# A fused audio-tower layer on one core: another order of work at the end, and one expert's weights loaded at another place

## The chip, the cores and the metric

The kernel runs on one core of one Trainium2 chip. The metric is the device time of one execution in microseconds (us), taken as the median of a few runs. A profile of one execution, taken by the hardware profiler, stands beside it.

## The reference, cut to what matters

The input is 64 clips, each cut to 7 patches of 16 x 64 values, so there are 448 tokens. Three stages follow.

```
h = layernorm(layernorm(patches) @ W + b)                    # 448 x 512
h = h + bitlinear(silu(gate) * value)                        # 512 -> 2 x 1408 -> 512, quantised
x = layernorm(h);  p = softmax(x @ router.T);  top 8 of 32 experts, shares normalised
h = h + sum over the chosen experts e of  share_e * (silu(x @ wg_e) * (x @ wu_e)) @ wd_e   # 512 -> 192 -> 512
```

The output is `h`, 448 x 512 in f32.

## The kernel before, in words

All matrices of the experts are in f32. The 448 tokens lie as 4 groups (g = 0 to 3) of 112 partitions. The work on the five engines is written out by hand as five instruction streams; every dependence is a semaphore wait, and each engine takes its stream strictly in order. SyncE (SP) and ScalarE (ACT) each issue direct DMAs on their own queue; GpSimd (POOL) issues the indexed gathers and scatters.

**Start and middle.** Patches, the first product and the quantised layer (up to about 97 us) end in `residual(g)` and `row(g)`: the normalised row of each token is stored to a DRAM table `token_rows`, 544 values per token, of which the last 32 are the token's shares. SP stores the four groups' rows (L511), waits for the shares (`gate_ready`), stores these (L513), then waits for `z_done` and for the first transposed tile (`xt_done` 1, L515) and loads experts 10 and 11 (`load_expert`, L487). Expert weights are 1,280 KB for an even expert and 1,024 KB for an odd one; there are 12 slots, and slot 10 lies over the matrix and the transposed values that the last product of the quantised layer reads (`z_done` tells that it has). POOL waits for all stores to `token_rows` (`rows_out` at 96) and issues the first gather (L646), with which the expert stage begins.

**Expert stage.** For each expert t = 0 to 31 a tile of up to 128 tokens is gathered, transposed, put through gate, up and down products, and added by a scatter with accumulate (L661) to one of two DRAM tables, `sum0` for even and `sum1` for odd t. A scatter waits until the scatter before it to the same table has landed (`added[n]`). Tokens of an expert beyond 128 are kept in lists of 32, four lists in a "quad", two quads a and b in a round. There is one round here (`n_pairs` is at least 1, and the loop of `pairs_of` runs once). The quads come after tile 31: PE does their products (L1186, L1218, L1220), ACT copies the result of each to SBUF (`y_list_out`, L892), and PE adds them into token order in PSUM by a product with a 0/1 matrix (`spread_lists`, L1243), a bank per group.

**The end before.** ACT's order in the round is: silu of both quads; wait until `added[0]` is complete, load all of `sum0` to SBUF (L917); wait until `added[1]` is complete, load all of `sum1` (L917); only then `y_list_out(a)` and `y_list_out(b)`. PE's `spread_lists` needs both copies in the order a, b within each group. DVE (VectorE) then does three adds for each group: `grown(g)` (L1751: h += PSUM bank g), `with_first(g)` (L1756: sum0 + h) and `finished(g)` (L1761: that + sum1 into `result`). SP stores groups 0 to 2 of the output and ACT group 3 (L446). PE's and ACT's work for a next round (`transpose_x`, `x_turned`) also stands at the end of the round.

Of the kernel before, what the change touches and what calls it, by code (L numbers as in the profile page):

```python
# [118 lines left out]
def program(nc, x, w_tok, vecs, gb1, w_in, w_down, g_down, w_router, ffn, out):  # L119
# [3 lines left out]
    with ctx:  # L123
# [3 lines left out]
        def sem(name):  # L127
            return ctx.enter_context(nc.semaphore(name))
# [141 lines left out]
        def bank(b, n=1):  # L270
            return ps[:, b:b + n, :].rearrange("p b c -> p (b c)")
# [60 lines left out]
        ld_rest = [sem(f"ld_rest{n}") for n in range(R)]  # L332
        ld_got = [sem(f"ld_got{n}") for n in range(8)]
        added = [sem(f"added{n}") for n in range(2)]
        ld_part = [sem(f"ld_part{n}") for n in range(2)]

        dve_chain = sem("dve_chain")
        pool_chain = sem("pool_chain")
# [66 lines left out]
        where_ready = sem("where_ready")  # L405
        spread_done = sem("spread_done")
        y_last = sem("y_last")
        with_h_ready = sem("with_h_ready")
        h_ready = sem("h_ready")

        place_done = sem("place_done")
# [11 lines left out]
        y_ready = sem("y_ready")  # L423
        fin_ready = sem("fin_ready")
        out_done = sem("out_done")
        act_out_done = sem("act_out_done")

        block = ctx.enter_context(nc.Block())
        ABS_COLS = (slice(0, 8), slice(8, 8 + DC))
# [9 lines left out]

        def bcast(v, n):  # L440
            return v.rearrange("(a n) -> a n", a=1).broadcast_to([G, n])

        def store(eng, g, n_pairs, done):

            eng.wait_ge(fin_ready, 4 * n_pairs + g)
            eng.dma_start(out_v[:, g, :], result[:, g, :]).then_inc(done, 16)  # L446


        @block.sync
        def _(sp):  # L450
            def load_x(g):
                sp.dma_start(xt[:, g, :], x_v[:, g, :]).then_inc(ld_x[g], 16)

            def load_down_piece(m):
                a, b = DOWN_PART[m], DOWN_PART[m + 1]
                sp.dma_start(w_down_raw[:, a:b, :], wdown_v[:, a:b, :]).then_inc(ld_wdown[m], 16)

            load_x(0)
            for n in range(2):
                sp.dma_start(raw_flat[:, n * 4 * D:(n + 1) * 4 * D],  # L460
                             w_tok.rearrange("(p c) n -> p (c n)", c=KC)[:, n * 4 * D:(n + 1) * 4 * D]
                             ).then_inc(ld_wtok[n], 16)
            for g in range(1, NG):
                load_x(g)

            def load_in_piece(n):
                a, b = WIN_PART[n], WIN_PART[n + 1]
                sp.dma_start(w_in_raw[:, a:b, :], win_v[:, a:b, :]).then_inc(ld_win[n], 16)

            for n in range(4):  # L470
                load_in_piece(n)
            for m in range(4):
                load_down_piece(m)
            sp.dma_start(gdn_bc[:, :], bcast(g_down, I1)).then_inc(ld_late, 16)
            sp.dma_start(rw_t[:, :, :], w_router.rearrange("p (c e) -> p c e", c=DC)).then_inc(ld_late, 16)
            sp.wait_ge(consts, 1)
            sp.dma_start(rows_dram[TOK:ROWS, :], zeros[:, :]).then_inc(rows_out, 16)
            for n in range(2):
                sp.dma_start(acc_dram[n][TOK:ROWS, :], zeros[:, 0:D]).then_inc(sums_ready, 16)
            for n in range(2):  # L480
                for g in range(NG):
                    sp.dma_start(acc_dram[n][g * G:(g + 1) * G, :], zeros[0:G, 0:D]).then_inc(sums_ready, 16)

            def load_expert(t):

                n, cols = t % R, WCOLS if t % 2 == 0 else WG + D
                sp.dma_start(slots[n][:, 0:cols], ffn[t, :, 0:cols]).then_inc(ld_gu[n], 16)  # L487

            def load_picked(e, n):

                sp.dma_start(slots[n][:, 0:WG + D], ffn[e, :, 0:WG + D]).then_inc(ld_gu[n], 16)
                sp.dma_start(down_rest_of(n), ffn[e, 0:IB, WG + D:WCOLS]).then_inc(ld_rest[n], 16)

            sp.wait_ge(t1_done, NG)
            load_expert(0)
            for t, signs in ((1, 3), (2, 5), (3, 8)):
                sp.wait_ge(wt_ready, signs)
                load_expert(t)
            sp.wait_ge(wd_ready, DC)
            for t in (4, 5, 6):  # L500
                load_expert(t)
            sp.wait_ge(swg_ready, gained(NG - 1))
            sp.wait_ge(swg_rest_ready, 1)
            sp.wait_ge(ssq2_ready, NG)
            load_expert(7)
            load_expert(8)
            sp.wait_ge(q2t_done, NG + 1)
            load_expert(9)
            for g in range(NG):
                sp.wait_ge(row_ready, g + 1)  # L510
                sp.dma_start(rows_v[:, g, 0:D], rows[:, g, 0:D]).then_inc(rows_out, 16)  # L511
            sp.wait_ge(gate_ready, NG)
            sp.dma_start(rows_v[:, :, D:ROW], rows[:, :, D:ROW]).then_inc(rows_out, 16)  # L513
            sp.wait_ge(z_done, NG)
            sp.wait_ge(xt_done, 1)  # L515
            load_expert(10)
            load_expert(11)
            for t in range(R, NE):
                sp.wait_ge(y_done, t - R + (1 if t % 2 else 2))
                load_expert(t)  # L520
            for k, n_pairs in pairs_of(sp, pairs_i, table_ready):
                for n in range(NLIST):
                    s = (NE + n) % R
                    e = sp.value_load(owner_row[0:1, bass.ds(NLIST * k + n, 1)], min_val=0, max_val=NE - 1)
                    sp.wait_ge(y_done, R * k + (NE - R + n + 1))
                    load_picked(bass.ds(e, 1), s)
            for g in range(NG - 1):
                store(sp, g, n_pairs, out_done)
            sp.wait_ge(out_done, 16 * (NG - 1))


        @block.gpsimd
        def _(pool):
# [144 lines left out]
            for k, n_pairs in pairs_of(pool, pairs_i, table_ready):  # L678
                for i in range(2):
                    gather(Quad(k + 1, i))  # L680
            for i in range(2):
                pool.wait_ge(ld_got[i], 16 * n_pairs + 16 * (NE // 8 + 1))

# [2 lines left out]
        def _(act):  # L686
# [222 lines left out]
            for k, n_pairs in pairs_of(act, pairs_i, table_ready):  # L909
                two = [Quad(k, 0), Quad(k, 1)]  # L910
                for m in two:
                    act.wait_ge(gu_done, m.lists(3))
                    silu(m)
                act.wait_ge(fin_ready, 4 * k + 3)
                for m in two:
                    act.wait_ge(added[m.i], 16 * (NE // 2))
                    act.dma_start(part[m.i][:, :, :], acc_v[m.i]).then_inc(ld_part[m.i], 16)  # L917
                for m in two:
                    y_list_out(m)
                for i in range(2):  # L920
                    x_turned(Quad(k + 1, i))
            store(act, NG - 1, n_pairs, act_out_done)
            act.wait_ge(act_out_done, 16)


        @block.tensor
        def _(pe):
# [307 lines left out]

            def spread_lists(two):

                for g in range(NG):
                    for m in two:
                        if g == 0:  # L1240
                            pe.wait_ge(y_ready, m.upto(-1))
                            pe.wait_ge(where_ready, 2 * m.k + (m.i + 1))
                        last = nc.tensor.matmul(bank(g)[0:G, :], where[:, m.i, g * G:(g + 1) * G], y_list[:, m.i, :],  # L1243
                                                start=m.i == 0, stop=m.i == 1)
                    last.then_inc(spread_done, 1)

            def list_starts():

# [76 lines left out]
        def _(dve):  # L1325
# [376 lines left out]
            for t in range(NE):  # L1702
# [13 lines left out]
                if t == 8:  # L1716
                    list_sought()
                    for i in range(2):
                        pick_lists(Quad(0, i))
                    nc.vector.tensor_copy(pairs_f[:, :], pairs_i[:, :]).then_inc(fin_ready, 3)  # L1720
                    dve.sem_inc(h_ready, 4)
                if t % 2 == 0:
                    turn_back(m)
# [6 lines left out]
            for k, n_pairs in pairs_of(dve, pairs_i, table_ready):  # L1730
# [19 lines left out]
                    dve.wait_ge(spread_done, 4 * k + (g + 1))  # L1750
                    nc.vector.tensor_tensor(h[:, g, :], h[:, g, :], bank(g)[0:G, :], ALU.add).then_inc(h_ready, 1)  # L1751

                def with_first(g):
                    dve.wait_ge(ld_part[0], 16 * k + 16)
                    dve.wait_ge(h_ready, 4 * k + (g + 5))
                    nc.vector.tensor_tensor(part[0][:, g, :], part[0][:, g, :], h[:, g, :], ALU.add).then_inc(with_h_ready, 1)  # L1756

                def finished(g):
                    dve.wait_ge(ld_part[1], 16 * k + 16)
                    dve.wait_ge(with_h_ready, 4 * k + (g + 1))  # L1760
                    nc.vector.tensor_tensor(result[:, g, :], part[0][:, g, :], part[1][:, g, :], ALU.add).then_inc(fin_ready, 1)  # L1761

                grown(0)
                with_first(0)
                grown(1)
                with_first(1)
                grown(2)
                with_first(2)
                finished(0)
                finished(1)  # L1770
                grown(3)
                with_first(3)
                finished(2)
                finished(3)


def laid_out(x, w_tok, b_tok, g1, b1, g2, b2, w_in, g_in, w_down, g_down, w_router, we_gate, we_up, we_down):
# [37 lines left out]
```

## Time and profile before

| | |
|---|---|
| median of 3 runs | 301.75 us |
| lowest, highest | 301.51, 305.46 us |
| the profiled execution, its own time | 302.17 us |
| its span, first to last instruction | 300.4 us |
| busy share of the span: TensorE, VectorE, ScalarE, GpSimd | 93%, 50%, 42%, 43% |
| mean granted TensorE clock over the span | 0.981 |

The span leaves out 1.77 us of the profiled execution's own time. A busy share is an average over stages that are limited by different things, so the stage at the end has to be read by its own rows. Times in the rows count from the start of the span.

### The profile page before, as it was taken

The numbers are of one execution on the slowest core, as the hardware profiler recorded it, in microseconds if no ns is written. First come the engines' busy times: TensorE is split into PE (matmuls) and PEld (weight loads), VectorE is DVE, ScalarE is ACT, GpSimd is POOL, SyncE is SP. The second block draws the span as 40 slices with busy tenths as digits, with TensorE's granted clock in tenths as the row PEclk, the third lists the DMA queues.
The fourth block names the chain that finished last, engine by engine and source line by source line (L and its number), as shares of the span: only waits on it lengthen the run. The fifth ranks groups of instructions, "written<-read, shape, count | busy, mean of one in ns | idle before, by whom it ended". The sixth has DMA issues, their size and how long they took to land.

```text
span 300.4 us, 3845 instructions
## 1 busy us (share of the span) xinstructions
PE 278.0 (93%) x1159; PEld 147.6 (49%) x1159; DVE 151.1 (50%) x446; ACT 125.2 (42%) x213; POOL 127.7 (43%) x130
## 2 busy tenths in 40 slices
PE   4899999869999988999999999999999999999792
PEld 1335444536557445546545655565555545553131
DVE  2657999997798705263343332333243223114345
ACT  2346999899984412213321332133213321331101
POOL 3162210976542133253546445654366436434400
PEclk9999999999999599999999999999999999999979
DMA  7999999501979087599999999999999999966773
GB/s 241 319 412 422 378 406 333 245 0 38 422 280 324 14 268 271 176 303 280 305 311 344 326 341 344 371 336 347 345 365 323 336 303 324 331 122 96 139 176 125
DMA packets 19478, 83.67 MB, mean 279 GB/s; under 512 B 3476, under 2 KB 3604, under 8 KB 13345
## 3 DMA queue, kind: packets, MB, share of 16 engines
q1 hardware_dynamic: 11440, 64.77, 57.5%
q0 software_dynamic: 7488, 16.58, 24.6%
q10 hardware_dynamic: 530, 2.08, 2.7%
q8 instruction: 10, 0.16, 0.2%
q14 instruction: 10, 0.08, 0.1%
HBM read 72.34 MB, written 12.92 MB: 284 GB/s over the span
## 4 chain that ended last, share of the span: by engine, by line
PE 35%; DMA 26%; DVE 18%; issue 5%; ACT 4%; POOL 1%; POOLq 0%; DVEq 0%; ACTq 0%
DMA sum<-w_t,add_idx 22%; PE ps L1174 16%; PE ps L1202 5%; PE ps L1195 3%; PE ps L1205 3%; DMA ring<-sum 3%; DVE big L1456 2%; DVE stats L1340 2%; PE ps L1061 2%; DVE raw L1462 2%; PE ps L1227 1%; DMA scrap<-token_rows,idx 1%; PE ps L1158 1%; DVE scrap L1421 1%; ACT last L814 1%
## 5 line engine op out<-in xcount | busy, mean ns | idle before, releaser
L661 POOL DMA_INDIRECT sum<-w_t,add_idx x32 | 51.3, 1602 | 55.6 <-ACT w_t L888 40.9
L877 ACT ACTIVATE w_t<-ps 128x512 f32<-128x512 f32 x36 | 21.3, 598 | 76.3 <-PE ps L1195 76.1
L648 POOL DMA_INDIRECT scrap<-token_rows,idx x28 | 29.5, 1053 | 28.6 <-DVE add_idx L1647 13.9
L1657 DVE COPY w_t<-ps 128x256 f32<-128x256 f32 x34 | 14.4, 424 | 53.6 <-PE ps L1230 52.4
L1652 DVE SCALAR_TENSOR_TENSOR w_t<-ps,scrap,w_t 128x192 f32<-128x192 f32 x32 | 13.2, 413 | 54.1 <-issue 44.9
L882 ACT ACTIVATE w_t<-ps 128x192 f32<-128x192 f32 x34 | 11.3, 331 | 54.2 <-PE ps L1174 48.8
L1174 PE MATMUL ps<-ring,w_t 128*128 128x384 f32 x96 | 33.1, 487 | 0.7 <-ACT w_t L877 0.7
L566 POOL TENSOR_TENSOR root_out<-root_in,minus_half 112x1 f32<-112x1 f32 x20 | 13.1, 654 | 46.6 <-DVE root_in L1357 46.6
L965 PE MATMUL ps<-raw,last 128*112 128x512 f32 x64 | 31.3, 643 | 0.0
L1174 PE MATMUL ps<-big,w_t 128*128 128x384 f32 x88 | 30.2, 486 | 0.0
L1195 PE MATMUL ps<-ident,scrap 128*128 128x128 f32 x144 | 23.0, 284 | 2.1 <-DVE h L1751 1.8
L1195 PEld LDWEIGHTS ps<-ident,scrap 128*128 128x128 f32 x144 | 21.1, 206 | 7.3 <-issue 6.0
L1174 PEld LDWEIGHTS ps<-ring,w_t 128*128 128x128 f32 x96 | 17.4, 192 | 10.4 <-ACT w_t L877 0.9
L1638 DVE SCALAR_TENSOR_TENSOR hit<-ps,iota_p,token 128x448 f16<-128x448 f32 x32 | 21.6, 676 | 1.4 <-PE ps L1263 1.0
L1023 PE MATMUL ps<-w_t,scrap 128*112 128x512 bf16 (+1 forms) x96 | 20.5, 363 | 1.7 <-DVE raw L1462 1.2
L888 ACT ACTIVATE w_t<-ps 128x512 f32<-128x512 f32 x31 | 17.4, 597 | 9.1 <-PE ps L1205 5.5
L965 PEld LDWEIGHTS ps<-raw,last 128*112 128x112 f32 x64 | 11.8, 192 | 18.4 <-issue 18.4
L1174 PEld LDWEIGHTS ps<-big,w_t 128*128 128x128 f32 x88 | 16.0, 191 | 8.7
L577 POOL TENSOR_TENSOR big<-raw,scrap 112x704 f32<-112x704 f32 (+1 forms) x7 | 12.7, 1825 | 8.7 <-DVE raw L1462 8.7
L1023 PEld LDWEIGHTS ps<-w_t,scrap 128*112 128x112 bf16 x96 | 11.9, 130 | 8.5 <-DVE raw L1462 1.4
L646 POOL DMA_INDIRECT scrap<-token_rows,idx x8 | 7.8, 979 | 17.5 <-DVE idx L1641 10.5
L723 ACT ACTIVATE scrap<-big 128x1536 bf16<-128x1536 f32 (+1 forms) x8 | 11.0, 1378 | 6.7 <-DMA big<-in_mlp_w_in 6.2
(216 smaller groups left out, 472.7 us busy)
## 6 DMA issues: line engine op xcount, KB each, us to landing
big<-in_ffn SPq DMA_DIRECT2D x12, 1024.0 KB, 9.3
ring<-in_ffn SPq DMA_DIRECT2D x9, 1280.0 KB, 7.5
ring<-in_ffn SPq DMA_DIRECT2D x4, 1024.0 KB, 9.9
raw<-in_ffn SPq DMA_DIRECT2D x4, 1024.0 KB, 9.0
last<-in_ffn SPq DMA_DIRECT2D x4, 1024.0 KB, 10.1
big<-in_ffn SPq DMA_DIRECT2D x3, 1280.0 KB, 8.0
big<-in_mlp_w_in SPq DMA_DIRECT2D x2, 1536.0 KB, 18.1
big<-in_mlp_w_in SPq DMA_DIRECT2D x2, 1280.0 KB, 20.7
```

Source lines behind the costliest of these rows:

```text
L648: nc.gpsimd.indirect_dma_start(got[:, got_at(s), :], None, rows_dram[:, :], rows_, bounds_check=TOK - 1, oob_is_err=False).then_inc(ld_got ...
L661: nc.gpsimd.indirect_dma_start(acc_dram[m.two][:, :], bass.IndirectOffsetOnAxis(ap=add_idx[:, m.eight:m.eight + 1], axis=0), y[:, m.four, ...
L877: nc.scalar.activation(x_t[:, m.two, :, :], bank(2 + m.two).rearrange("p (c t) -> p c t", c=4), ACT.Copy).then_inc(xt_ready, 1)
L888: nc.scalar.activation(y[:, m.four, :], bank(4 + m.two), ACT.Copy).then_inc(y_ready, 1)
L965: last = nc.tensor.matmul(acc, patch_t[g % 2][:, c, :], wtok_raw[:, c, :], start=False, stop=c == KC - 1)
L1023: last = nc.tensor.matmul(bank(3 * half_, 3)[0:G, a:a + w], q1_t[:, c, g * G:(g + 1) * G], w_t4[:, c, half_ * I1 + a:half_ * I1 + a + w], ...
L1174: last = nc.tensor.matmul(dst, x_t[:, m.two, c, :], wg[:, :, c, :], start=c == 0, stop=c == 3)
L1195: last = nc.tensor.transpose(bank(2 + m.two)[:, c * P:(c + 1) * P], got[:, got_at(m.eight), c:D:4], ident[:, :])
L1202: nc.tensor.matmul(bank(4 + m.two), h_t[:, m.two, 0, :], down_of(m.slot), start=True, stop=False)
L1638: nc.vector.scalar_tensor_tensor(hit[:, :], bank(b)[:, 0:TOK], mine, token[:, :], ALU.is_equal, ALU.mult, accum_out=idx_f[:, s:s + 1]).the ...
L1652: nc.vector.scalar_tensor_tensor(hid[:, m.two, 0:IE], bank(m.two)[:, IE:2 * IE], gate, sg[:, :], ALU.mult, ALU.mult).then_inc(hid_ready, 1)
L1657: nc.vector.tensor_copy(h_t[:, m.two, :, :], bank(6)[:, 0:2 * P].rearrange("p (c t) -> p c t", c=2)).then_inc(ht_ready, 1)
```

## The change

Five things are different.

1. ACT no longer waits for the sums and no longer loads them: after silu it goes to `y_list_out(a)` and `y_list_out(b)`.
2. SP loads the sums, in four pieces of 224 KB for each table (one per group), after `added[n]` is complete. Each piece has its own semaphore, `ld_part[n][g]`.
3. POOL adds the two sums for each group (part0 + part1), once both pieces of that group have landed and after its last two gathers. DVE does `grown(g)` for all four groups, and after the round, for each group, one add of POOL's sum and h into `result`. All four stores of the output are SP's.
4. PE's spreading takes the products in the order (group, quad) = (0,a) (1,a) (0,b) (2,a) (1,b) (3,a) (2,b) (3,b), in place of a, b for each group in turn.
5. SP waits for `z_done` and loads expert 10 after the four row stores, ahead of the wait for the shares, their store and the wait for `xt_done`. Expert 11 stays behind `xt_done`.

A small DVE copy that made up the count of `fin_ready` at tile 8 is gone.

```diff
@@ SP
             for g in range(NG):
                 sp.wait_ge(row_ready, g + 1)
                 sp.dma_start(rows_v[:, g, 0:D], rows[:, g, 0:D]).then_inc(rows_out, 16)
+            sp.wait_ge(z_done, NG)
+            load_expert(10)
             sp.wait_ge(gate_ready, NG)
             sp.dma_start(rows_v[:, :, D:ROW], rows[:, :, D:ROW]).then_inc(rows_out, 16)
-            sp.wait_ge(z_done, NG)
             sp.wait_ge(xt_done, 1)
-            load_expert(10)
             load_expert(11)
...
-            for g in range(NG - 1):
-                store(sp, g, n_pairs, out_done)
-            sp.wait_ge(out_done, 16 * (NG - 1))
+            for n in range(2):
+                sp.wait_ge(added[n], 16 * (NE // 2))
+                for g in range(NG):
+                    sp.dma_start(part[n][:, g, :], acc_v[n][:, g, :]).then_inc(ld_part[n][g], 16)
+            for g in range(NG):
+                sp.wait_ge(fin_ready, g + 1)
+                sp.dma_start(out_v[:, g, :], result[:, g, :]).then_inc(out_done, 16)
+            sp.wait_ge(out_done, 16 * NG)
@@ POOL
+            for g in range(NG):
+                for n in range(2):
+                    pool.wait_ge(ld_part[n][g], 16)
+                nc.gpsimd.tensor_tensor(part[0][:, g, :], part[0][:, g, :], part[1][:, g, :], ALU.add).then_inc(both_ready, 1)
@@ ACT
-                act.wait_ge(fin_ready, 4 * k + 3)
-                for m in two:
-                    act.wait_ge(added[m.i], 16 * (NE // 2))
-                    act.dma_start(part[m.i][:, :, :], acc_v[m.i]).then_inc(ld_part[m.i], 16)
                 for m in two:
                     y_list_out(m)
...
-            store(act, NG - 1, n_pairs, act_out_done)
-            act.wait_ge(act_out_done, 16)
@@ PE
-                for g in range(NG):
-                    for m in two:
-                        if g == 0:
...
+                for g, i in ((0, 0), (1, 0), (0, 1), (2, 0), (1, 1), (3, 0), (2, 1), (3, 1)):
+                    m = two[i]
+                    if g == 0:
...
+                    if m.i == 1:
+                        last.then_inc(spread_done, 1)
@@ DVE
-                grown(0)
-                with_first(0)
-                grown(1)
-                with_first(1)
-                grown(2)
-                with_first(2)
-                finished(0)
-                finished(1)
-                grown(3)
-                with_first(3)
-                finished(2)
-                finished(3)
+                for g in range(NG):
+                    grown(g)
+            for g in range(NG):
+                dve.wait_ge(both_ready, g + 1)
+                dve.wait_ge(h_ready, 4 * n_pairs + (g + 1))
+                nc.vector.tensor_tensor(result[:, g, :], part[0][:, g, :], h[:, g, :], ALU.add).then_inc(fin_ready, 1)
```

## Rows read from the trace of the kernel before

**Rows 1.** The page's head.

```profile
span 300.4 us, 3845 instructions
```

**Rows 2.** Chain that ended last, 260 to 301 us: start, length, what.

```profile
276.94 4.81 DMA sum<-w_t,add_idx
...
281.83 8.06 DMA ring<-sum
...
293.86 0.69 DVE raw L1761
```

**Rows 3.** Timeline, 281.5 to 301 us: start, length, engine, line, operation, [idle before, releaser].

```profile
281.83 2.17 ACTq L917 DMA_DIRECT2D ring<-sum  x2
...
282.52 0.34 PE L1165 MATMUL ps<-w_t,pick 32*128 32x448 f16 x1
...
284.05 1.08 ACT L892 ACTIVATE scrap<-ps 128x512 f32<-128x512 f32 x2 [5.94 <-DMA sum<-w_t,add_idx]
...
284.77 8.81 PE L1243 MATMUL ps<-scrap,ranked 128*112 128x512 f32 x16 [1.91 <-ACT scrap L892]
284.94 1.04 POOL L648 DMA_INDIRECT scrap<-token_rows,idx  x1 [2.21 <-DVE idx L1641]
...
287.66 0.69 DVE L1751 TENSOR_TENSOR h<-h,ps 112x512 f32<-112x512 f32 x1 [3.68 <-PE ps L1243]
...
295.78 1.28 DVE L1761 TENSOR_TENSOR raw<-ring 112x512 f32<-112x512 f32 x2
...
297.10 0.33 ACTq L446 DMA_DIRECT2D out<-raw  x1
```

**Rows 4.** L917, the loads of the sums: issues, then time to landing.

```profile
L917 ACTq DMA_DIRECT2D ring<-sum x2: 320/336/351, 281.8 to 283.7; - x2
...
DMA to landing us min/median/max: 8.1/8.6/9.1
```

**Rows 5.** L446, the four stores of 224 KB to the output: time to landing.

```profile
DMA to landing us min/median/max: 2.3/2.8/3.0
```

**Rows 6.** Windows: stretch, length, PE, PEld, DVE, ACT, POOL busy, PEclk, DMA share, GB/s.

```profile
284.00:286.00 2.00, 1.23 (x3) 0.73 (x4) 0.00 (x0) 1.08 (x2) 1.04 (x1) 0.93 0.93 275
286.00:288.00 2.00, 2.00 (x3) 0.64 (x3) 0.34 (x1) 0.00 (x0) 0.00 (x0) 0.50 0.90 213
288.00:290.00 2.00, 2.00 (x5) 0.68 (x4) 0.35 (x2) 0.00 (x0) 0.00 (x0) 0.72 1.02 266
```

**Rows 7.** GpSimd's adds or products of two SBUF tensors: L577, durations in ns.

```profile
L577 POOL TENSOR_TENSOR big<-raw,scrap x7: 1671/1683/2315, 61.6 to 81.8; 112x704 f32<-112x704 f32 x6, 112x640 f32<-112x640 f32 x1
```

**Rows 8.** Timeline at 61 to 66 us and at 82 us: GpSimd and VectorE beside each other.

```profile
61.56 3.69 POOL L577 TENSOR_TENSOR big<-raw,scrap 112x704 f32<-112x704 f32 x2 [0.23 <-DVE raw L1462]
...
63.60 1.93 DVE L1437 TENSOR_SCALAR scrap<-scrap,fscale 112x512 f32<-112x512 f32 x1
...
81.81 0.96 DVE L1476 TENSOR_TENSOR big<-raw,scrap 112x768 f32<-112x768 f32 x1
...
81.85 2.31 POOL L577 TENSOR_TENSOR big<-raw,scrap 112x640 f32<-112x640 f32 x1 [3.65 <-DVE raw L1462]
```

**Rows 9.** Timeline, 89 to 109 us: SP's queue and the first gather.

```profile
89.93 6.46 SPq L511 DMA_DIRECT2D token_rows<-scrap  x4
...
100.32 0.72 SPq L513 DMA_DIRECT2D token_rows<-scrap  x1
...
103.51 1.21 POOL L646 DMA_INDIRECT scrap<-token_rows,idx  x1 [7.76 <-DVE idx L1641]
...
108.03 0.83 SPq L487 DMA_DIRECT2D last<-in_ffn  x2
```

**Rows 10.** L513, the store of the shares: time to landing.

```profile
DMA to landing us min/median/max: 2.2/2.2/2.2
```

**Rows 11.** Windows around SP's stores, columns as in rows 6.

```profile
88.00:90.00 2.00, 1.91 (x20) 1.25 (x19) 1.73 (x6) 1.91 (x4) 0.55 (x1) 1.00 1.00 411
98.00:100.00 2.00, 1.96 (x10) 0.97 (x10) 1.57 (x10) 0.88 (x5) 0.00 (x0) 0.50 0.02 8
```

More of the change, by code:

```diff
@@ L334, in program @@
         added = [sem(f"added{n}") for n in range(2)]
-        ld_part = [sem(f"ld_part{n}") for n in range(2)]
+        ld_part = [[sem(f"ld_part{n}_{g}") for g in range(NG)] for n in range(2)]
         dve_chain = sem("dve_chain")
@@ L407, in program @@
         y_last = sem("y_last")
-        with_h_ready = sem("with_h_ready")
+        both_ready = sem("both_ready")
         h_ready = sem("h_ready")
@@ L425, in program @@
         out_done = sem("out_done")
-        act_out_done = sem("act_out_done")
         block = ctx.enter_context(nc.Block())
@@ L441, in bcast @@
             return v.rearrange("(a n) -> a n", a=1).broadcast_to([G, n])
-        def store(eng, g, n_pairs, done):
-            eng.wait_ge(fin_ready, 4 * n_pairs + g)
-            eng.dma_start(out_v[:, g, :], result[:, g, :]).then_inc(done, 16)
         @block.sync
@@ L1236, in spread_lists @@
             def spread_lists(two):
-                for g in range(NG):
-                    for m in two:
-                        if g == 0:
[L1241 to L1245, printed above, removed]
+                for g, i in ((0, 0), (1, 0), (0, 1), (2, 0), (1, 1), (3, 0), (2, 1), (3, 1)):
+                    m = two[i]
+                    if g == 0:
+                        pe.wait_ge(y_ready, m.upto(-1))
+                        pe.wait_ge(where_ready, 2 * m.k + (m.i + 1))
+                    last = nc.tensor.matmul(bank(g)[0:G, :], where[:, m.i, g * G:(g + 1) * G], y_list[:, m.i, :],
+                                            start=m.i == 0, stop=m.i == 1)
+                    if m.i == 1:
+                        last.then_inc(spread_done, 1)
             def list_starts():
@@ L1719, in _ @@
                         pick_lists(Quad(0, i))
-                    nc.vector.tensor_copy(pairs_f[:, :], pairs_i[:, :]).then_inc(fin_ready, 3)
                     dve.sem_inc(h_ready, 4)
@@ L1751, in grown @@
                     nc.vector.tensor_tensor(h[:, g, :], h[:, g, :], bank(g)[0:G, :], ALU.add).then_inc(h_ready, 1)
[L1753 to L1761, printed above, removed]
-                grown(0)
-                with_first(0)
-                grown(1)
-                with_first(1)
-                grown(2)
-                with_first(2)
-                finished(0)
-                finished(1)
-                grown(3)
-                with_first(3)
-                finished(2)
-                finished(3)
+                for g in range(NG):
[4 more added lines that the diff above has]
+                nc.vector.tensor_tensor(result[:, g, :], part[0][:, g, :], h[:, g, :], ALU.add).then_inc(fin_ready, 1)
 def laid_out(x, w_tok, b_tok, g1, b1, g2, b2, w_in, g_in, w_down, g_down, w_router, we_gate, we_up, we_down):
```

## The prediction, written before the result was known

> **What bounds the kernel now.** I read the page's head first, then the chain that ended last for the final 40 us, then the timeline of the same stretch, and last the windows and the DMA rows. The span is 300.4 us [rows 1]. The chain at the end shows that no compute engine sets it: a scatter issued at 276.94 lands at 281.75, the load of the first sum is issued at 281.83 and lands 8.06 us later at 289.89, and then DVE adds one after the other [rows 2]. The second load is issued at 283.7 and lands 9.1 us later, at 292.8 [rows 4]. DVE's last add ends at 297.06, ACT's store is issued at 297.10 [rows 3], lands about 2.9 us later [rows 5], and 0.4 us are left to the end. So from 281.8 on the path is: sums from DRAM, what is left to add, a store. The spreading runs beside it. PE finishes the quads' products at 282.86 but starts spreading at 284.77, since ACT sat 5.94 us and copied the first quad only at 284.05 [rows 3]. That is the wait which the change takes away, and it lies beside the loads, not ahead of them.
>
> **Part 1, ACT's wait goes (copies and spreading).** The spreading starts at about 282.9, when PE is through, 1.9 us earlier [rows 3]. With the new order quad b is wanted first after two products, 2 x 8.81/8 = 2.2 us later at most, and ACT's copy, half of the 1.08 us that two take, is long done. The eight products took 8.81 us, of which the clock was at the low level for 3.4 us: the windows show 0.93, 0.50 and 0.72 over 6 us [rows 6], a loss of 1.7 us. Ahead of the fall PE had stood idle 1.9 us, which now goes, so I take the full level: 7.1 us, done at 290.0 (low level again: 291.7). `grown(3)` follows with 0.1 + 0.69 us [rows 3], at 290.8 (292.5). Gain on the path: nothing, as long as the sums come later. It is a floor, though: the final adds stand behind `grown(3)` in DVE's order, four at 0.69 us make 293.6 (295.3), and 0.1 for SP's reaction, 2.9 for the store and 0.4 to the end give 297.0 (298.7). No saving of more than 3.4 us can come of the end.
>
> **Part 2, the loads in pieces on SP.** The releasers are the same scatters at the same times, so piece 0 of sum0 still goes out at 281.8 and piece 0 of sum1 at 283.7. SP's direct DMAs cost about 0.35 us each to issue (ACT's 0.32 to 0.35 [rows 4]), four take 1.4 us and fit between the two. What decides is when piece (1,0), the fifth of eight, lands. Early bound: 283.7 + 2.6, as a store of this size takes alone [rows 5], 286.3. Late bound: the bytes keep the pace of before, half in at 289.89 and all at 292.8, so the fifth eighth at 289.89 + 2.9/4 = 290.6 [rows 2, 4]. Between: from 284 to 290 the queues moved 275, 213 and 266 GB/s, mean 251 [rows 6]; five pieces of 224 KB (1.147 MB) take 4.6 us, from 284.0, so 288.6. I take 288.6, for it is these bytes in this stretch without the wait for later bytes of the same load.
>
> The Trainium skill, "DMA: Bandwidth & Descriptors", section "Measured (HBM→SBUF, 128 partitions, SWDGE, issued from GpSimd)", speaks against pieces: it asks for 1 MiB or more in a DMA and shows 64 KB at 138 GB/s where 1 MB has 341. What I weigh of it here is that the loads of 896 KB were no faster than 251 GB/s either, while 224 KB stores landed in 2.3 to 3.0 us. By the page the pieces would land nearer the late bound, about 2 us more than my sum.
>
> **Part 3, GpSimd adds the sums.** POOL is free at 286.0, after its last gather [rows 3]. Products of two SBUF tensors of 704 columns took 1.683 us in the median [rows 7], 2.39 ns a column, so 1.22 us for 512, and 4.9 us for four. They run beside DVE's final adds, which read two SBUF tensors as well. Once in the trace the two met like this: POOL's 640 columns beside a DVE add of 0.96 us took 2.31 us in place of 1.53, 0.78 more [rows 8]. For a DVE add of 0.69 us that is 0.56, and three of them overlap: 1.7 us (bounds 0 and 3 x 0.69 = 2.1). DVE can lose as well: a 512-column operation took 1.93 us beside two POOL products [rows 8].
>
> Sum from the landing of piece (1,0): 0.1 reaction + 4.9 + 1.7 + 0.1 + 0.69 (DVE's last) + 0.1 (SP) + 2.9 + 0.4 = 10.9 us. 288.6 + 10.9 = 299.5 against 300.4: 0.9 us less. Late bound 290.6 + 10.9 = 301.5, early bound the floor of part 1.
>
> The Trainium skill, "SBUF — State Buffer", section "SBUF: two separate sides", calls this an exclusive lock: whichever of the two starts first holds the pair for its whole instruction. The 0.78 us beside a 0.96 us DVE add, and DVE's 1.93 us, are on its side. By it DVE's four final adds could all come behind POOL's four, 4.9 + 4 x 0.69 = 7.7 where I have 7.4 with the last add, 0.3 us more.
>
> **Part 4, expert 10 sooner.** SP has issued the fourth row store at 96.4 [rows 9], `z_done` is past by then (the fourth row is made from the residual that waited for it), so the load goes out there, behind the stores on the same queue. These are through by 98: the window 98 to 100 shows 8 GB/s [rows 11]. 1.31 MB at the 411 GB/s of 88 to 90 take 3.2 us, until 101.2. The store of the shares, issued at 100.32, landed 2.2 us later [rows 9, 10]; it now starts up to 0.9 us late if it had begun at once, and hardly late if its 0.72 us of issue and its start filled that time. POOL's first gather came 1.0 us after that landing [rows 9, 10], so a delay goes straight to it and to everything after. I take 0.1 us. Bounds: 0, and 2.0 if the load moves only at the 251 GB/s of part 2, 5.2 us, to 103.2, where the store would else have begun by 101.2. What it gives back: 1,280 KB fewer at 108, where PE waits for no DMA; nothing. SP's issue, 0.4 us, fits before the shares are ready at 100.3. The DVE copy that is gone has one element, and DVE is no bound there: nothing.
>
> **Sum.** -0.9 + 0.1 = -0.8 us on the profiled execution's 302.17, which is 0.42 above the median of 301.75. Predicted median: 300.9 us.
>
> **Rivals.**
> - *Forecast*, the pieces in the middle, GpSimd's adds the path: 299.5 to 302, chance 0.50.
> - *Fast pieces.* The pieces land near 286.5 to 287 and POOL and DVE don't collide: 287 + 9.2 = 296.2, so the floor decides, 297.0, or 298.7 at the low clock. Then the gain is 3.4 or 1.7 us: 298.3 or 300.0. For it: 224 KB stores alone land in 2.6 us. Against: the loads of before were slow from a queue that was busy 0.90 to 1.02 of the time [rows 6]. Chance 0.25.
> - *Slower: GpSimd becomes the end.* Piece (1,0) at 290.6 and POOL's adds at its dearest row, 2.31/640 a column, 1.85 us each: 7.4 in place of 6.6, so 301.5 + 0.8 = 302.3, 1.9 us above: 303.6. It decides as soon as piece (1,0) lands later than 289.5 with the collision as summed, since the rest takes 10.9. Chance 0.17.
> - *Shares behind the load.* The gather waits 2.0 us and takes back more than the end gives: 301.75 - 0.9 + 2.0 = 302.8; chance 0.08. By the same skill page, section "Queues, rings and completion order", SP's DMAs share rings and are taken in order, which the wait for the load's bytes here rests on.
>
> That the change does not do what it says is hardly open: ACT's wait stands ahead of both copies in its stream, and it is gone.
>
> **Range and chances.** The range 298.3 to 303.2 reaches from the floor at full clock to just under the slower rival's far end, and leaves out about 2 in 10. A measurement of this kernel can tell some 2% (6 us) from no change. Faster by over 2% would need an end before 294.4, below the floor: 0.03. Slower by over 2% needs both slow rivals and more: 0.03. Within 2%: 0.94.
>
> **What would show it.** Right: ACT's copies done by 283.3 with no DMA wait; spreading from 282.9 to 290; SP issuing eight loads between 281.8 and 285.2, with piece (1,0) landing near 288.6; POOL adds of 1.2 to 1.8 us; SP's last store near 296.1; the first gather near 103.6. Wrong: a spreading that ends after 291 or keeps the low clock (part 1), POOL adds above 2 us or waiting on pieces past 290 (parts 2, 3), DVE's final adds bunched behind POOL's last (the lock), the first gather past 104 (part 4), or tiles that take another time than before, which I hold unchanged.

## The result and the profile after

The changed kernel is **0.8% slower**: the ratio of comparable runs is 1.0084, 95% interval [1.0047, 1.012], which on 301.75 us is 2.5 us (1.4 to 3.6). The median of 20 runs was 305.5 us against 301.8 for the kernel before, one beside the other; single runs of either scatter over 7 us. (The ratio leaves disturbed executions out, the medians do not, which is why they lie further apart; the profiles of the first and third experiments below are of such disturbed executions, so their distances are read only beside those of others.) The forecast was 300.9 us, range 298.3 to 303.2, so both the sign and the range were missed.

The profiled execution of the changed kernel took 302.52 us, span 300.5, so beside [rows 1] it hardly shows the loss: this execution happened to be 1.2 us ahead already at 88 us, before anything that was changed. Spans of single executions are therefore no measure here. What follows compares *distances between two events of one execution*: from the issue of the load (or first piece) of sum1 to the end of the span, and from the index of the first tile to the first gather.

The chain of waits that ended last, from 276 us (start, length, what), answers to [rows 2]:

```profile
278.50 4.60 DMA sum<-w_t,add_idx
283.11 0.02 issue
283.12 5.54 DMA ring<-sum
...
288.80 1.28 POOL ring L682
...
290.27 1.10 DVE raw L1754
...
291.77 1.28 DVE raw L1754
...
293.44 1.27 DVE raw L1754
294.72 0.09 issue
294.80 0.99 DVEq L123
```

The first piece of sum1 landed at 283.12 + 5.54 = 288.66 (forecast 288.6), GpSimd began its adds 0.14 us later, and VectorE followed. The timeline of the same stretch (start, length, engine, line, operation), answering to [rows 3]:

```profile
280.42 0.60 ACT L894 ACTIVATE scrap<-ps 128x512 f32<-128x512 f32 x1 [2.60 <-PE ps L1216]
280.92 4.11 SPq L523 DMA_DIRECT2D ring<-sum  x8
...
282.41 0.60 ACT L894 ACTIVATE scrap<-ps 128x512 f32<-128x512 f32 x1 [1.39 <-PE ps L1216]
282.51 0.27 PEld L1239 LDWEIGHTS ps<-scrap,ranked 128*112 128x112 f32 x2 [0.21 <-issue]
...
288.80 5.83 POOL L682 TENSOR_TENSOR ring<-ring 112x512 f32<-112x512 f32 x4 [3.10 <-DMA ring<-sum]
...
289.67 0.69 DVE L1747 TENSOR_TENSOR h<-h,ps 112x512 f32<-112x512 f32 x1 [0.17 <-PE ps L1239]
290.27 5.52 DVE L1754 TENSOR_TENSOR raw<-ring,h 112x512 f32<-112x512 f32 x4
...
291.87 4.26 SPq L526 DMA_DIRECT2D out<-raw  x4
```

ScalarE's two copies wait for TensorE alone, and the spreading starts at 282.51, as soon as TensorE is through with its products: the first copy has been there since 281.02. Single lines: the loads in pieces, the stores, GpSimd's adds and VectorE's last adds (durations in ns, min/median/max, first to last start; then the time to landing), which answer to [rows 4, 5, 7]:

```profile
L523 SPq DMA_DIRECT2D ring<-sum x8: 303/427/620, 280.9 to 284.4; - x8
...
DMA to landing us min/median/max: 3.8/5.5/6.2
...
L526 SPq DMA_DIRECT2D out<-raw x4: 317/320/323, 291.9 to 295.8; - x4
...
DMA to landing us min/median/max: 2.3/2.3/2.6
...
L682 POOL TENSOR_TENSOR ring<-ring x4: 1267/1492/1715, 288.8 to 292.9; 112x512 f32<-112x512 f32 x4
...
L1754 DVE TENSOR_TENSOR raw<-ring,h x4: 678/1658/1749, 290.3 to 295.1; 112x512 f32<-112x512 f32 x4
```

The last store was issued at 295.82 and landed 2.6 us later, at 298.4. Yet the span ends at 300.5. What stands there is seen only when the instructions of the closing line L123 are asked for on GpSimd:

```profile
L123 POOLq COMPARE_BRANCH  x1: 41/41/41, 290.8 to 290.8; - x1
L123 POOLq DRAIN  x1: 9286/9286/9286, 291.0 to 291.0; - x1
```

and, the same two lines of the kernel before:

```profile
L123 POOLq COMPARE_BRANCH  x1: 41/41/41, 293.1 to 293.1; - x1
L123 POOLq DRAIN  x1: 5626/5626/5626, 293.2 to 293.2; - x1
```

Each of the five engines has such a DRAIN at the end of its stream, and in all 13 profiles of this text the span ends 0.21 to 0.25 us after the last of the five is over, whichever engine's that is. Before, GpSimd's DRAIN took 5.63 us and ended at 298.88, 1.5 us ahead of the end of the span. Now it starts while GpSimd's adds still run and ends at 300.29, which is 5.66 us after the end of the last add (294.63) and 0.2 us before the end of the span. SyncE's waits (us in all, times, longest) say the same from the other side, under its own closing line: after its last store has landed it waits 1.9 us for the others, where it waited 0.7 before. Where no closing of GpSimd stands in the way (the third, sixth, seventh, eighth, ninth and tenth experiments), 0.4 us lie between the last landing and the end of the span.

```profile
SPq L123 <- DMA out<-raw: 2.2, 1, 2.2
SPq L123 <- PEq L123: 1.9, 1, 1.9
```

Two more places, by windows (length; PE, PEld, VectorE, ScalarE, GpSimd busy; clock; DMA share; GB/s), which answer to [rows 6, 11]: first the load of expert 10 in its new place, then the end.

```profile
96.00:98.00 2.00, 1.84 (x10) 1.78 (x11) 1.20 (x9) 1.09 (x7) 0.00 (x0) 0.50 1.01 306
98.00:100.00 2.00, 1.63 (x10) 0.57 (x8) 1.51 (x10) 0.98 (x4) 0.00 (x0) 0.50 0.95 399
100.00:102.00 2.00, 1.78 (x5) 0.57 (x6) 1.16 (x4) 1.64 (x3) 0.00 (x0) 0.50 0.27 63
...
284.00:286.00 2.00, 2.00 (x6) 0.78 (x5) 0.62 (x1) 0.00 (x0) 1.04 (x1) 1.00 0.90 268
286.00:288.00 2.00, 2.00 (x6) 0.89 (x5) 0.76 (x2) 0.00 (x0) 0.00 (x0) 1.00 0.92 282
...
290.00:292.00 2.00, 1.23 (x8) 1.04 (x8) 2.00 (x3) 0.64 (x2) 2.00 (x3) 1.00 0.00 1
```

The queues, which before moved 8 GB/s from 98 to 100, now move 399, and the store of the shares, issued at 99.67 into this, lands later than the 2.2 us of [rows 10]. Expert 10's load, issued at 95.24, lands at 102.19, the shares at 102.56 and the first gather starts at 103.51. The load, and then the store:

```profile
L480 SPq DMA_DIRECT2D last<-in_ffn x1: 429/429/429, 95.2 to 95.2; - x1
...
DMA to landing us min/median/max: 7.0/7.0/7.0
```

```profile
L508 SPq DMA_DIRECT2D token_rows<-scrap x1: 715/715/715, 99.7 to 99.7; - x1
...
DMA to landing us min/median/max: 2.9/2.9/2.9
```

### The profile page after: what moved, and what is told of

Same layout as the page of the kernel before. It is cut to its first block, busy times and chain, and to the rows that moved or that the text cites. A ratio compares the mean times of both kernels' runs of the same rounds, so it can differ in the third digit from the quotient of the medians.

```text
span 300.5 us, 3841 instructions
## 1 busy us (share of the span) xinstructions
PE 276.6 (92%) x1159; PEld 147.5 (49%) x1159; DVE 151.4 (50%) x441; ACT 125.1 (42%) x213; POOL 133.7 (44%) x134
## 4 chain that ended last, share of the span: by engine, by line
DMA 36%; PE 24%; DVE 18%; issue 6%; ACT 4%; POOL 2%; DVEq 0%; POOLq 0%; ACTq 0%
DMA sum<-w_t,add_idx 34%; PE ps L1170 10%; PE ps L1198 3%; DVE big L1453 2%; DVE stats L1337 2%; PE ps L1191 2%; DMA ring<-sum 2%; PE ps L1201 2%; PE ps L1057 2%; PE ps L936 2%; DVE raw L1459 2%; DVE raw L1754 1%; ACT w_t L890 1%; DVE scrap L1418 1%; ACT last L816 1%
## 5 line engine op out<-in xcount | busy, mean ns | idle before, releaser
L884 ACT ACTIVATE w_t<-ps 128x192 f32<-128x192 f32 x34 | 11.3, 331 | 54.9 <-PE ps L1170 49.7
L961 PE MATMUL ps<-raw,last 128*112 128x512 f32 x64 | 30.2, 624 | 0.0
L644 POOL DMA_INDIRECT scrap<-token_rows,idx x8 | 7.8, 981 | 18.6 <-DVE idx L1638 11.3
```

What stands on the lines that cost most here:

```text
L961: last = nc.tensor.matmul(acc, patch_t[g % 2][:, c, :], wtok_raw[:, c, :], start=False, stop=c == KC - 1)
```

## The experiments

Two theories stood against each other for the loss. **The closing of GpSimd:** its late adds push its DRAIN past the last store. **The shares:** the store waits behind expert 10's bytes, and the whole expert stage starts later. Times are ratios to the kernel before on the same chip, with 95% intervals; "end" is the distance from the issue of sum1's first load to the start of the span's last instruction, 0.05 us before the end of the span (before: 16.67 us; changed: 17.36, and 17.19 in a second profile), "start" is from the end of the operation that makes the first tile's index on VectorE to the first gather (before: 1.11 us; changed: 1.76 and 2.06).

**Expert 10 back in its old place, the rest as changed.**

```diff
-            sp.wait_ge(z_done, NG)
-            load_expert(10)
             sp.wait_ge(gate_ready, NG)
             sp.dma_start(rows_v[:, :, D:ROW], rows[:, :, D:ROW]).then_inc(rows_out, 16)
+            sp.wait_ge(z_done, NG)
             sp.wait_ge(xt_done, 1)
+            load_expert(10)
```

> The changed kernel with one part undone: expert 10 is loaded where it was before, behind the first transposed tile; the new end is kept. Theory A (the load ahead of the shares' store held that store, 2.9 us to landing in place of 2.2, and with it the first gather by 0.7 us): faster than the changed kernel by about 0.7 us, the shares' store again 2.2 us to landing. Rival (the load's place is worth nothing, all of the loss is at the end): no difference to the changed kernel, first gather 1.8 us after the first index as there.

Measured: 0.9962 [0.991, 1.0013]; end 18.14, start 1.11, the store of the shares lands in 2.2 us again. The start is mended, and the end is not: GpSimd's last add and the DRAIN still close it (DRAIN until 304.86, span 305.1). The gain on the changed kernel's 1.0084 is 1.2 points, some 3.7 us on another chip, where 0.7 us was expected.

**The kernel before with only expert 10 moved.**

```diff
+            sp.wait_ge(z_done, NG)
+            load_expert(10)
             sp.wait_ge(gate_ready, NG)
             sp.dma_start(rows_v[:, :, D:ROW], rows[:, :, D:ROW]).then_inc(rows_out, 16)
-            sp.wait_ge(z_done, NG)
             sp.wait_ge(xt_done, 1)
-            load_expert(10)
```

> The kernel before with one part of the change alone: expert 10 loaded ahead of the wait for the shares. Theory A: about 0.7 us slower than before (302.5 where before is 301.8), with the shares' store landing 2.9 us after its issue. Rival: within 0.2 us of before.

Measured: 1.0013 [0.996, 1.0065]; start 1.40, the shares land in 2.5 us; end 16.99. In this profile the move costs 0.3 us by this distance, less than the 0.7 expected, and by time alone it cannot be told from nothing.

This run showed something about part 1 as well. It has ScalarE's wait and the same idle time ahead of the spreading (1.87 us; 1.91 in [rows 3]), but its clock did not fall, and the old order of the products took 7.12 us:

```profile
284.00:286.00 2.00, 1.32 (x3) 0.63 (x4) 0.00 (x0) 1.04 (x2) 1.04 (x1) 1.00 0.92 266
286.00:288.00 2.00, 2.00 (x6) 0.89 (x5) 0.69 (x1) 0.00 (x0) 0.00 (x0) 1.00 0.94 238
288.00:290.00 2.00, 2.00 (x6) 0.79 (x5) 0.00 (x0) 0.00 (x0) 0.00 (x0) 1.00 0.90 213
```

**As changed, but VectorE adds the two sums.**

```diff
@@ POOL
-            for g in range(NG):
-                for n in range(2):
-                    pool.wait_ge(ld_part[n][g], 16)
-                nc.gpsimd.tensor_tensor(part[0][:, g, :], part[0][:, g, :], part[1][:, g, :], ALU.add).then_inc(both_ready, 1)
@@ DVE
             for g in range(NG):
+                for n in range(2):
+                    dve.wait_ge(ld_part[n][g], 16)
+                nc.vector.tensor_tensor(part[0][:, g, :], part[0][:, g, :], part[1][:, g, :], ALU.add).then_inc(both_ready, 1)
                 dve.wait_ge(both_ready, g + 1)
```

> The changed kernel with the four adds of the two sums moved from GpSimd to VectorE, after the four adds of the spread products; all else as in the changed kernel. Theory B (the end waits for GpSimd's closing drain, which ends 5.66 us after GpSimd's last work, at 300.3, while the last store has landed by 298.1): with GpSimd free of the adds its drain starts when the last gathers have landed (about 290 to 291) and ends by 297; VectorE has eight adds of 0.69 us from 290.4, ends at 295.9, and the end is at about 298.7 where the changed kernel has 300.5, 1.8 us less. Rival C (only the collision of the two engines' adds costs, the drain is a record without effect): VectorE ends at 295.9 as it does now (295.8), so the end stays at 300.5, no difference.

Measured: 1.0005 [0.9956, 1.0054]; end 15.18, start 2.65. VectorE's last add ends 12.37 us after the issue of sum1's load, where it was 12.67 with GpSimd's help in the changed kernel: four adds more on VectorE cost no time there. They take 0.684 us each; beside GpSimd VectorE's adds took 1.66 and GpSimd's 1.49 in the median. And GpSimd's DRAIN is out of the way: issued at 299.11, over at 304.74, 1.5 us ahead of the end of the span.

```profile
L123 POOLq DRAIN  x1: 5626/5626/5626, 299.1 to 299.1; - x1
```

The start is the dearest seen. In this execution the bytes of expert 10 moved for longer after the store was issued, 236 GB/s from 100 to 102 where the profile of the changed kernel had 63; the load landed at 103.92, and the store, 3.8 us after its issue, at 104.26:

```profile
L508 SPq DMA_DIRECT2D token_rows<-scrap x1: 718/718/718, 100.5 to 100.5; - x1
...
DMA to landing us min/median/max: 3.8/3.8/3.8
```

**The kernel before with one late column on GpSimd.** One add of 112 x 1, which waits until VectorE has finished all four groups; its result is used by nothing.

```diff
@@ POOL
+            pool.wait_ge(fin_ready, 7)
+            nc.gpsimd.tensor_tensor(root_out[:, 0:1], root_in[:, 0:1], minus_half[:, :], ALU.add)
```

> The kernel before with one thing added: a one-column add on GpSimd (0.1 us, nobody reads it) that waits until three of the four final results are there, at about 296.5. Theory B: GpSimd's closing drain then ends about 5.6 us later, at 302.2 or more, and the kernel is some 2 us slower than before. Rival C: the tiny add is beside ScalarE's last store and the end stays where it is, no difference to before.

Measured: 1.0045 [0.9983, 1.0107]; end 19.83, 3.2 us more than before, for an add of 0.19 us. The timeline's last row and the closing line of GpSimd:

```profile
298.52 0.19 POOL L682 TENSOR_TENSOR root_out<-root_in,minus_half 112x1 f32<-112x1 f32 x1 [11.46 <-DVE raw L1763]
```

```profile
L123 POOLq DRAIN  x1: 5626/5626/5626, 298.8 to 298.8; - x1
```

The DRAIN ends at 304.44 and the span at 304.7. The duration is the same to the nanosecond as before and with VectorE's adds, though the last work ahead of it is one column here and a gather there. 5.73 us lie from the end of the add (298.71) to the end of the DRAIN, as 5.66 did behind the four large adds. So the size of the last work, 512 columns or one, made no difference of over 0.1 us. In the trace this settles the mechanism; in time the interval still holds 1.

**The changed kernel again, beside the next three.**

> The changed kernel once more, as it is, beside the others of this call. Theory B (GpSimd's closing drain sets the end): from the issue of the first load of sum1 to the end of the span 17 to 18 us again (17.4 in its first profile, 16.7 in the kernel before), and the drain's end within 0.3 us of the span's. Theory A: the first gather 1.4 us or more after the first index (1.1 in the kernel before).

Measured: 1.0052 [0.9998, 1.0107]; end 17.19, start 2.06, shares landing in 3.2 us. It agrees with the result.

**Both undone: expert 10 in its old place and VectorE adding the sums** (the edits of the first and the third experiment together).

> The changed kernel with both suspected costs gone: the sums are added by VectorE and not by GpSimd, and expert 10 is loaded at its old place. Theories A and B together: 1.5 us from load to end are won at the end (15.2 us as in the run with VectorE's adds alone, against 16.7) and the first gather comes 1.1 us after the first index, so about 1.5 us faster than before. Rival (the loss is somewhere in the expert stage, by another timing of its transfers): no faster than before.

Measured: 0.9897 [0.9829, 0.9965]; end 15.42, start 1.11. So what is left of the change (ScalarE's wait gone, loads and stores on SyncE, the new order of the products, none of them tried alone) is a gain, of 1.0% where about 1.5 us, 0.5%, was expected. The four variants form a square: changed 1.0052, without GpSimd's adds 1.0005, with expert 10 back 0.9962, with both 0.9897. Each edit gives 0.5 to 0.7% and 0.9 to 1.1%, whichever is made first (two of the four from another chip, so this is a reading of points whose intervals overlap).

**The loads whole.** The kernel before, with SyncE issuing both loads of 896 KB and all stores, ScalarE free of them, the new order of the products, and VectorE adding in the order four times `grown`, four times `with_first`, four times `finished`.

```diff
@@ SP
+                sp.wait_ge(fin_ready, 4 * k + 3)
+                for n in range(2):
+                    sp.wait_ge(added[n], 16 * (NE // 2))
+                    sp.dma_start(part[n][:, :, :], acc_v[n]).then_inc(ld_part[n], 16)
@@ ACT
-                act.wait_ge(fin_ready, 4 * k + 3)
-                for m in two:
-                    act.wait_ge(added[m.i], 16 * (NE // 2))
-                    act.dma_start(part[m.i][:, :, :], acc_v[m.i]).then_inc(ld_part[m.i], 16)
```

> The kernel before with ScalarE's wait gone and the new spreading order, but the sums loaded by SyncE in the two loads of 896 KB of before; VectorE does all adds, the four of the products first; expert 10 at its old place. It tells what the pieces are worth. If pieces land no earlier than their share of the whole (my late bound): the same as the run with VectorE's adds in pieces, 15.2 us from load to end. If whole loads land at 8.1 and 9.1 us as before and pieces sooner (5.5 to 6.6 us to the fifth piece in the traces so far): VectorE starts its eight adds at 6.2 us after that load's issue, ends at 11.8, and the end is at 14.7 us, so the pieces are worth nothing here.

Measured: 0.9895 [0.9826, 0.9964]; end 15.12. The two loads land in 7.7 and 8.6 us. That is as good as pieces with the sums added by VectorE (15.18 and 15.42), but the order of the adds differs too, so the pieces are not isolated. In this order they could give nothing: the adds of sum1 come last, from 292.80 on, and find the whole load landed at 292.2.

**Pieces, and VectorE's adds laid between.** As the last one, but with the four pieces of each load and the order grown 0, first 0, grown 1, first 1, grown 2, first 2, grown 3, finished 0, first 3, finished 1, 2, 3. The wait for the last gathers' landing goes from GpSimd to SyncE.

```diff
@@ SP
+                for n in range(2):
+                    sp.wait_ge(added[n], 16 * (NE // 2))
+                    for g in range(NG):
+                        sp.dma_start(part[n][:, g, :], acc_v[n][:, g, :]).then_inc(ld_part[n][g], 16)
+            for i in range(2):
+                sp.wait_ge(ld_got[i], 16 * (NE // 8 + 2))
@@ DVE
                 with_first(2)
-                finished(0)
-                finished(1)
                 grown(3)
+                finished(0)
                 with_first(3)
+                finished(1)
                 finished(2)
```

> The version the runs point to: pieces on SyncE, sum0 added to h by VectorE between the adds of the spread products, sum1 last, nothing on GpSimd after its last gather (the wait for that gather is SyncE's), expert 10 at its old place. Theory B: VectorE's last add ends 11.3 us after the first load of sum1 is issued, the end is at 14.2 us, 2.5 us less than before; GpSimd's drain starts when its last gather is issued and is over by 292. Rival C (the end follows the transfers alone, whoever adds): no better than the run with VectorE's adds behind the spreading.

Measured: 0.9847 [0.9768, 0.9925], from four executions; end 13.67, start 1.11. VectorE's timeline shows why it is shorter: the adds of sum0 fill its waits for TensorE, and only five are left behind the last `grown`.

```profile
288.59 0.69 DVE L1756 TENSOR_TENSOR ring<-ring,h 112x512 f32<-112x512 f32 x1
289.58 0.69 DVE L1751 TENSOR_TENSOR h<-h,ps 112x512 f32<-112x512 f32 x1 [0.30 <-PE ps L1242]
290.31 0.69 DVE L1756 TENSOR_TENSOR ring<-ring,h 112x512 f32<-112x512 f32 x1
290.92 0.68 DVE L1751 TENSOR_TENSOR h<-h,ps 112x512 f32<-112x512 f32 x1
291.51 0.69 DVE L1761 TENSOR_TENSOR raw<-ring 112x512 f32<-112x512 f32 x1
292.12 0.69 DVE L1756 TENSOR_TENSOR ring<-ring,h 112x512 f32<-112x512 f32 x1
292.72 1.89 DVE L1761 TENSOR_TENSOR raw<-ring 112x512 f32<-112x512 f32 x3
```

GpSimd's DRAIN ends at 293.97, 4.1 us before the end, and 2 us later than the 292 that was expected; it was not over until 2.83 us after the last gather had landed (291.14):

```profile
L123 POOLq DRAIN  x1: 8611/8611/8611, 285.4 to 285.4; - x1
```

**The same kernel on another chip, and with each suspect put back alone.**

> The best version so far (pieces on SyncE, all adds interleaved on VectorE, nothing late on GpSimd, expert 10 at its old place), as it is, with more runs. All theories: 0.98 to 0.99 of the time of the kernel before, about 13.7 us from the first load of sum1 to the end of the span.

Measured: 0.9878 [0.9816, 0.9939]; end 13.73, start 1.11. The version is 1.2 to 1.5% faster than the kernel before, on two chips, and so beats both kernels.

To it, expert 10's load was moved ahead of the shares (the edit of the second experiment):

> The best version with the one part of the change that is at the start of the expert stage: expert 10 loaded ahead of the shares' store. Theory A: the first gather comes 1.4 to 2.7 us after the first index (1.11 in the best version) and the kernel is 0.3 to 1.5 us slower than the best version. Rival (no cost): 1.11 us again, same time.

Measured: 0.9972 [0.9915, 1.0029]; start 1.92, shares landing in 3.1 us; end 13.88. The end is as good as without it, and most of the gain is gone, 0.94 points.

And to it, the one late column on GpSimd (the edit of the fourth):

> The best version with a one-column add on GpSimd (nobody reads it) that waits until three of the four final results are there. Theory B: GpSimd's closing drain ends 5.7 us behind that add, at about 300 where the best version ends at 298, and the stretch from the first load of sum1 to the end grows from 13.7 to about 16 us: 2 us slower. Rival C: no difference.

Measured: 1.0028 [0.9985, 1.0072]; start 1.11; end 16.59, 2.9 us more than the 13.73 beside it. The DRAIN, issued at 297.37, ends at 303.24, and the span at 303.5. Here the time shows it too: 1.5 points, with intervals that lie apart.

## Why the prediction was wrong, step by step

**What bounds the end: right as far as the last store.** From the landing of the first piece of sum1 to the issue of the last store I summed 7.6 us (0.1 + 4.9 + 1.7 + 0.1 + 0.69 + 0.1); it took 295.82 - 288.66 = 7.16.

**Part 1: right, with a reason too strong.** Spreading 282.51 to 289.63 at full clock, 7.12 us (forecast 282.9, 7.1, 290.0). But the idle time ahead of it does not by itself bring the fall of the clock: with 1.9 us of it the clock fell in the kernel before and in the fourth experiment and stayed up in the second. In the ten profiles without it the clock never fell there. That there is no gain on the path from this alone was right for the changed kernel. The floor was right as well: 297.0 was 13.3 us from the issue of sum1's load, and the eighth, ninth and tenth experiments, with VectorE's adds laid between, reached 13.67, 13.73 and 13.88.

**Part 2: right at the end, by some luck.** Piece (1,0) landed at 288.66, forecast 288.6. But its load went out at 283.12, 0.6 us sooner than I had it, and took 5.54 us where 4.9 was forecast (4.6 to 6.3 in the eight other profiles with pieces); the two errors cancel. The queues moved 268 and 282 GB/s from 284 to 288, where [rows 6] have 275 and 213. The rule of the Trainium skill, "DMA: Bandwidth & Descriptors", section "Measured (HBM→SBUF, 128 partitions, SWDGE, issued from GpSimd)", from which I had estimated that the pieces would cost about 2 us, is not borne out for these direct loads: the eight pieces had all landed 9.6 to 10.5 us after the first was issued (nine profiles), the two whole loads 10.7 to 11.3 us (four profiles).

**Part 3: the adds right, the end of the program left out. This is the step that failed.** GpSimd's first add took 1.27 us (forecast 1.22 alone), the four 5.83 (forecast 6.6 with collision); VectorE, not GpSimd, then paid for most of the collision. After 290, where both have work, both are busy the whole of 290 to 292, and VectorE's add goes from 0.68 to between 1.57 and 1.75 us. The Trainium skill, "SBUF — State Buffer", section "SBUF: two separate sides", describes an exclusive lock between the two; the trace agrees in kind. GpSimd's first two adds keep their 1.27 us, and VectorE's first, begun beside the second, takes 1.57 in place of 0.68; from then on the two engines take turns, GpSimd's adds 1.71 us and VectorE's 1.75, one pair every 1.67 us, a little less than the 1.27 + 0.68 = 1.95 us of the two alone. What failed is the phrase "2.9 for the store and 0.4 to the end". The store landed at 298.4, and by that phrase the end would have been at 298.8; it came at 300.5, because GpSimd's closing ran until 300.29. So up to the store the forecast gain was there: 15.7 us from the issue of sum1's load against 16.7 before. The closing took back 1.7 us. The row that tells of it stands in the trace of the kernel before: a DRAIN of 5626 ns that ended 1.5 us ahead of the end of the span. I had read [rows 3] and the chain [rows 2], and neither shows an instruction that is not counted as busy. From it the sum would have been: GpSimd's last add ends at 288.6 + 0.1 + 6.6 = 295.3, plus 5.6 and 0.2, gives 301.1 in place of 299.5, and thus a time 0.7 us above the profiled one. So the rival "GpSimd becomes the end" came true in sign, by another mechanism than its own: not dear adds but what follows the last of them.

**Part 4: mis-sized.** The shares' store was late by 0.7, 1.6, 1.0, 0.3 and 0.8 us in the five profiles with the early load (the changed kernel, the third, fifth, second and tenth experiments), on average 0.9, and the gather with it: in all 13 profiles it starts 0.94 or 0.95 us after the shares have landed. I had taken 0.1 with bounds of 0 and 2.0. I asked when the load's bytes would be through, and had 101.2 from the windows; what counted was when the load *landed*. That was 6.6 to 7.7 us after its issue, at 102.16 to 103.92, and the shares landed 0.33 to 0.37 us behind it in every one of the five. The rate in the window from 100 to 102 does not order the delays (63 GB/s with 2.9 us to landing, 212 with 2.5, 236 with 3.8, 405 with 3.1), the landing of the load does. The Trainium skill, "DMA: Bandwidth & Descriptors", section "Queues, rings and completion order", has descriptors of one ring taken in order; the constant 0.33 to 0.37 us agrees.

**The account.** End: 17.28 on average (17.36 and 17.19) against 16.67 and, in the second experiment, 16.99: +0.3 to +0.6 us, where -0.9 was forecast. Start: +0.65 and +0.95 us, where +0.1 was. Together 0.9 to 1.6 us of a measured 2.5 (1.4 to 3.6). Put into the forecast, GpSimd's closing alone makes 301.75 + 0.7 = 302.4, still inside the range; with 0.9 for the shares it is 303.3, just past its end at 303.2, and the measured ratio stands for 304.3. So the range was missed by both steps together and by something more. "Start" counts from an index that is itself late in some of these profiles. From the start of GpSimd's last one-column operation ahead of it (94.78 before, 93.58 changed) the first gather comes after 8.6 to 9.2 us in the eight profiles without the early load, on average 8.8, and after 9.6 to 10.7 in the five with it: 9.9 and 10.2 in those of the changed kernel. Counted so, the start costs 1.1 and 1.4 us and the whole 1.4 to 2.0. About 0.3 us of it lie ahead of the issue of the shares' store, and no run shows that the load causes them. The end is shown in trace and, on the best version, in time. Of the start, the lateness of the shares behind the load is shown; but putting the early load back costs some 1% in three comparisons of ratios (0.9, 1.1 and 0.9 points, about 2.9 us, each interval wide), two to three times what the gather was late, and 0.1% in the comparison within the kernel before. From the first gather to sum1's load the profiles with the early load took 179.6 to 185.9 us and those without 180.2 to 183.7, so the traces show no further loss and cannot exclude one of 1 to 2 us. This stays open.

## What to carry to other kernels

Ask each engine's closing instructions, not only its busy ones, how long they take: here GpSimd's last add, of 512 columns or of one, fixes the earliest end of the program 5.9 to 6.0 us later, so nothing late belongs on it, and a free engine is not free there. Before giving work to a second engine to relieve VectorE, look whether VectorE's own waits hold it: twelve adds laid between those waits were done 10.2 to 10.6 us after the issue of sum1's load, eight beside GpSimd after 12.5 to 13.5. And do not put a large load ahead of a small store that a whole stage waits for, even if the queue is empty for those microseconds: the store landed only behind the load.

## What the runs showed of the hardware that I had not expected

- **GpSimd's closing DRAIN lasts 5.63 us** when the engine was idle (5626 ns in the kernel before and in five of the experiments), and ends 5.66 us after the last add when it was issued while adds still ran (three profiles). Behind a last gather, with no wait for its landing, it ended 2.83 us after the gather had landed (three profiles).
- **Moving the wait for a landing off GpSimd** lets its closing run early: with the wait on SyncE the DRAIN was over 2.83 us after the last gather had landed (at 293.97), with it on GpSimd 5.9 us after (at 298.88 in the kernel before).
- **The fall of TensorE's clock in the spreading** (0.93, 0.50 and 0.72 before) came in the kernel before and in the one with the late column, not in the second experiment with the same code there, and in no kernel in which the spreading followed directly on the quads' products.
- **A small store behind a large load on SyncE** landed after 2.5 to 3.8 us in place of 2.2, always 0.33 to 0.37 us behind the landing of the load.
